# A new order for the slots of the first layer: lane transpositions, gates by Tanh, the middle layer's bank and the routing's norm

## The chip, the core and the metric

The kernel runs on one core of a Trainium2 chip. A core has a matrix engine (TensorE, PE in the profile; PEld is its weight load, which overlaps), VectorE (DVE), ScalarE (ACT), GpSimd (POOL) and SyncE (SP), each with an instruction stream of its own that it works off in order; semaphores tie the streams together. The metric is the time of one execution on the device in microseconds.

## The reference

The input is 4096 tokens of 128 numbers in float32. They pass two layers. Cut to what matters:

```python
# first layer
x = x + 0.5 * L0_ffn(layernorm(x))      # experts in LoRA form over shared weights
x = x + L0_attn(layernorm(x))
x = x + 0.5 * L0_ffn(layernorm(x))
# second layer
x = x + 0.5 * L1_ffn(layernorm(x))      # every token goes to one of 8 experts
x = x + L1_attn(layernorm(x))
x = x + 0.5 * L1_ffn(layernorm(x))

# L0_ffn: softmax over 8 experts, the best two; for each of them
h1 = t @ w1.T + 2 * (t @ a1[e].T) @ b1[e].T
h3 = t @ w3.T + 2 * (t @ a3[e].T) @ b3[e].T
act = silu(h1) * h3                     # weighted by the expert's share
out_e = act @ w2.T + 2 * (act @ a2[e].T) @ b2[e].T

# L0_attn: a recurrence along the sequence
h = layernorm(x) * g1 + b1;  f = sigmoid(h @ Wf + bf);  i = sigmoid(h @ Wi + bi)
o = sigmoid(h @ Wo + bo);    v = h @ Wv + bv
num = scan(f * num + i * v); den = scan(f * den + i)
x = x + o * num / (den + 1e-6)
m = square(leaky_relu((layernorm(x) * g2 + b2) @ W1 + b1));  x = x + m @ W2 + b2
```

(The reference writes the recurrence as an exponential of summed logarithms; the program computes it with scans.)

## The kernel before

The tokens lie in 8 chunks of 512. The first layer is a pipeline of slots (`Slot`, lines 52 to 63, `SLOTS`). Slot m does, for different chunks, one stage of each of many lanes. The main lane has 16 items, the 8 chunks for the first L0_ffn and again for the second: item m is `main` in slot m, `pre` (`q`, the transposition, the gate logits, the choice of the best two, the masks and the lane products `up`) in the slot before, `stat` two before, `tail` (`l`) one after. The attention's lanes lag: `a_stat` (slot m - 1), `a_pre`, `a_gate`, `a_norm`, `a_up`, `a_down` (m - 6) for chunks 0 to 7. The routing of the second layer lags more: `r_stat` (m - 9), `r_pre` (m - 10), `r_sort` (m - 11). So slots 0 to 2 hold only L0_ffn work beside statistics, slots 3 to 10 gates, 5 to 12 the middle layer, and 9 to 18 routing. Slots -2 and -1 fill the pipeline, 16 to 18 empty it; `fill` and `keep_busy` put products there whose results nobody uses.

Inside a slot the order of each engine is written out by hand: `first_layer(s)` stands once in each engine's block and ends with a list of calls. On TensorE, `h(1, k)` and `h(3, k)` (lines 362 to 364) are the products for h1 and h3, k = 1 to 8 for four column blocks and two experts, each of three or six split float32 products of 512 columns, which read `split` (the high and low halves of a float32). `value` (L421) is the product with `a2`, `down` (L431) the one with `w2`, `pre_T` (L358, `yn_f`), `logits` (L459), `mask` (L473, L476), `up` (L362) and `a_T` (L358, `yn_a`) belong to the lanes. `a_gate(i)` (L609) is one of four products of `hT` with the weights of i, f, o and v, all into one bank, `BSIDE`: gate i + 1 waits until gate i has been read. `a_den` (L502) and `a_back` (L358, `oaT`) belong to the attention of the slot before.

ScalarE applies Silu (L863), copies masks (L903), makes the high halves (`up_high`, L914), and reads the gates with Sigmoid (`a_gates`, L971). Its functions come from tables, and a change of table is an ACT_TABLE_LOAD. VectorE makes `act` (L1199, then L1203 by the expert's weight), `f_norm` (L1212: `yn_f`, at the head of the slot, for `q`), `masked` (L1266 and L1267: `ua`, `ud`), `a_leaky` (L1342), `a_scans` (L1360, L1361, L1363: `den`, `iv`, `num`) and the chains of small instructions for statistics, best two and routing. GpSimd adds the two experts' act (`total`, L1644), makes low halves (`low`, L1631; `up_low`, L1672), `mdT` (L1664), the inverse roots, `a_product` (L1709) and the scatter of the routing.

BSIDE (bank 5) is also the bank of the attention's transpositions, of `a_mid` (L573, the middle layer) and of the routing's affinities and ranks; BV (bank 4) holds `value` and the routing's transposition `r_T`; BPRE (bank 7) holds the lane's.

## Time and profile before

| | us |
|---|---|
| median of 3 runs | 1057.73 |
| lowest and highest | 1056.75, 1062.28 |
| the profiled execution | 1054.69 |
| its span, first to last instruction | 1053.0 |
| of it the first layer's slots | 0 to 684 |

The profile is of one execution, 3.0 us under the median. A row of its timeline is: start, length, engine, line, operation, output<-input, count, and in brackets how long the engine had been idle before it and what ended that. Matmuls are pipelined: the shown length of one overlaps the next, so the distance of two starts is the better measure of what one costs.

### The profile page before, as it was taken

How to read it: one execution, taken by the hardware profiler on the slowest of the kernel's cores; microseconds unless marked ns; L12 is line 12 of the kernel's file. 1: busy time of each engine (PE TensorE's matmuls, PEld its weight loads, DVE VectorE, ACT ScalarE, POOL GpSimd, SP SyncE). 2: the span in 40 equal slices, each digit the busy share in tenths (PEclk: the TensorE clock that was granted, in tenths of full speed). 3: DMA queues.
4: the chain of work that ended last, by engine and by line, in shares of the span. 5: the costliest groups of instructions: out<-in, count | busy, mean ns of one | idle time of the engine just before them, and what ended most of it. 6: DMA issues, size and time to landing. Idle time of an engine off the chain costs nothing. (4 is left out here: it accounts for less than half of the span.)

```text
span 1053.0 us, 15574 instructions
## 1 busy us (share of the span) xinstructions
PE 980.6 (93%) x4429; PEld 669.9 (64%) x4429; DVE 711.2 (68%) x2140; ACT 507.9 (48%) x1039; POOL 500.1 (47%) x485
## 2 busy tenths in 40 slices
PE   3999999999999999999999999899988999889993
PEld 2766667656565665656566656477864667648873
DVE  5787779788786877879797776445543667634542
ACT  3433454655646556564453332144534777515451
POOL 3456555554535545354654655524451155423443
PEclk9999999999999999999999999999999999989997
DMA  6069000000000000000000002146534000015651
GB/s 181 1 284 415 3 1 1 1 1 1 1 0 2 0 1 1 1 0 1 12 3 9 11 11 71 39 137 197 166 94 140 1 22 22 22 42 178 194 174 34
DMA packets 42900, 65.12 MB, mean 62 GB/s; under 512 B 7153, under 2 KB 25121, under 8 KB 40640
## 3 DMA queue, kind: packets, MB, share of 16 engines
q1 hardware_dynamic: 37824, 55.59, 16.1%
q0 software_dynamic: 4992, 8.54, 2.4%
q8 instruction: 36, 0.59, 0.2%
q14 instruction: 48, 0.39, 0.1%
HBM read 37.20 MB, written 28.74 MB: 63 GB/s over the span
## 5 line engine op out<-in xcount | busy, mean ns | idle before, releaser
L362 PE MATMUL bank<-split 128*128 128x512 f32 x416 | 206.9, 497 | 7.8 <-DVE ud L1267 4.1
L364 PE MATMUL bank<-split 128*128 128x512 f32 x416 | 165.2, 397 | 0.0
L363 PE MATMUL bank<-split 128*128 128x512 f32 x416 | 164.8, 396 | 0.0
L863 ACT ACTIVATE sil<-bank 128x512 f32<-128x512 f32 x128 | 76.2, 595 | 116.0 <-PE bank L364 115.2
L1644 POOL TENSOR_TENSOR gsum<-act 128x512 f32<-128x512 f32 x64 | 84.9, 1327 | 81.5 <-DVE act L1203 81.4
L421 PE MATMUL bank<-act,a 128*128 128x512 f32 x256 | 117.6, 592 | 0.0
L362 PEld LDWEIGHTS bank<-split 128*128 128x128 f32 x416 | 79.5, 191 | 48.8 <-issue 17.4
L1199 DVE TENSOR_TENSOR act<-bank,sil 128x512 f32<-128x512 f32 x128 | 87.8, 686 | 17.2 <-PE bank L364 14.2
L363 PEld LDWEIGHTS bank<-split 128*128 128x128 f32 x416 | 79.9, 192 | 28.3 <-issue 18.6
L688 PE MATMUL bank<-xlT,e 128*128 128x256 f32 x368 | 91.2, 392 | 5.1 <-ACT xlT L1068 2.7
L1203 DVE TENSOR_TENSOR act<-act,wT 128x512 f32<-128x512 f32 x128 | 91.7, 716 | 4.4
L364 PEld LDWEIGHTS bank<-split 128*128 128x128 f32 x416 | 79.2, 190 | 18.1
L704 PE MATMUL bank<-hT_e,e 128*128 128x256 f32 x368 | 87.3, 380 | 1.1 <-DVE oT_e L1534 1.1
L1068 ACT ACTIVATE xlT<-bank,lnb,lng 128x256 f32<-128x256 f32 x46 | 25.9, 564 | 119.0 <-PE bank L696 119.0
L1747 POOL DMA_INDIRECT rows_in<-yw,slot_i x64 | 62.9, 983 | 34.7 <-issue 18.8
L688 PEld LDWEIGHTS bank<-xlT,e 128*128 128x128 f32 x368 | 67.9, 194 | 16.5 <-issue 4.5
L1754 POOL DMA_INDIRECT out<-ob,ids x46 | 45.2, 983 | 66.9 <-DVE ob L1542 57.1
L1754 POOL DMA_INDIRECT rows_out<-ob,ids x46 | 45.2, 983 | 63.4 <-DVE ob L1542 55.6
L421 PEld LDWEIGHTS bank<-act,a 128*128 128x128 f32 x256 | 47.5, 190 | 42.0 <-issue 33.7
L704 PEld LDWEIGHTS bank<-hT_e,e 128*128 128x128 f32 x368 | 66.7, 191 | 8.7 <-issue 1.5
L431 PE MATMUL bank<-gsum,w 128*128 128x512 f32 x128 | 65.2, 600 | 0.5 <-POOL gsum L1644 0.5
L1529 DVE TENSOR_SCALAR hT_e<-bank,eb1T 128x256 f32<-128x256 f32 x92 | 40.3, 479 | 27.6 <-PE bank L688 27.2
(283 smaller groups left out, 1957.6 us busy)
## 6 DMA issues: line engine op xcount, KB each, us to landing
e<-e_dram SPq DMA_DIRECT2D x92, 256.0 KB, 3.1
rows_in<-yw SPq DMA_DIRECT2D x17, 1056.0 KB, 17.8
xin<-rows_in SPq DMA_DIRECT2D x46, 132.0 KB, 3.0
x<-rows_out SPq DMA_DIRECT2D x8, 256.0 KB, 4.7
rows_in<-yw,slot_i POOLq DMA_INDIRECT x64, 2.3
rows_out<-ob,ids POOLq DMA_INDIRECT x46, 2.3
out<-ob,ids POOLq DMA_INDIRECT x46, 2.4
act<-b_dram SPq DMA_DIRECT2D x2, 256.0 KB, 3.1
```

Source lines behind the costliest of these rows:

```text
L362: mm(dst, w[0], m[0], start=start, stop=False, **more)
L363: mm(dst, w[0], m[1], start=False, stop=False, **more)
L364: return mm(dst, w[1], m[0], start=False, stop=stop, **more)
L421: last = mm(bank[BV][:, :], a2[:, j, :], act_[e][j][:, :], start=j == 0, stop=j == J - 1)
L431: mm(bank[BOUT][:, :], w2[:, j, :], gsum[j % 2][:, :], start=j == 0, stop=False).then_inc(w2_used.sem, 1)
L688: last = mm(bank[2 * p + j // 2][:, (j % 2) * Q:(j % 2 + 1) * Q], w[:, rows(j)], xlT[p][:, :], start=True, stop=True)
L704: last = mm(bank[4][:, 0:Q], w[:, j, :], hT_e[p][:, j, :], start=j == 0, stop=j == J - 1)
L863: af(sil[(k - 1) % 2][:, :], bank[BH1[STEPS[k - 1][0] % 2]][:, :], ACT.Silu).then_inc(silu_done.sem, 1)
L1199: v.tensor_tensor(a[:, :], bank[BH3[j % 2]][:, :], sil[(k - 1) % 2][:, :], ALU.mult).then_inc(act_done.sem, 1)
L1203: v.tensor_tensor(a[:, :], a[:, :], wT[g % 2][e][:, :], ALU.mult).then_inc(weighted.sem, 1)
L1644: pool.tensor_tensor(out=gsum[j % 2][:, :], in0=act_[0][j][:, :], in1=act_[1][j][:, :], op=ALU.add).then_inc(summed.sem, 1)
L1754: pool.indirect_dma_start((rows_out, o)[n3 // NT], bass.IndirectOffsetOnAxis(ids[n3 % 4][:, q:q + 1], 0), ob[n3 % 4][:, q, :], None, bound ...
```

## The change

The lists of calls at the end of `first_layer` are written in a new order on all four engines, with the waits that this needs; three functions change.

- TensorE: `pre_T` between h(1,1) and h(3,1), `logits` after h(1,2), `a_den` after h(3,2), `a_back` after `value(1)`. The masks and the gates are spread over h(3,5) to h(3,8); `up(0)` after h(1,7), `up(1)` after h(1,8). `down(2)` and `down(3)` now end the slot, with no gates between them.
- The middle layer (`a_mid_T`, `a_mid`) moves from BSIDE to BV, the routing's `r_T` from BV to BSIDE. `r_T` then waits for what held BSIDE, `a_mid_T` for `r_done`; `value(0)` waits for `m_saved`, `r_rank` and `a_gate(0)` for `xnT_saved`.
- ScalarE: `a_gates` becomes `a_gate(i)`, called three times: the gate is 0.5 * tanh(0.5 * (z + b)) + 0.5, a Tanh out of the bank and a Copy in place. The halved biases are made once (`half`). `r_norm` of chunk n stands in slot n + 10 instead of n + 9, but for the last chunk.
- VectorE: `f_norm` leaves the head of the slot, works on `stat` and stands after act(8) and `a_leaky(1)`, so at the end of the slot before. `masked(0)` stands before act(7) and `masked(1)` before act(8). `r_rows` follows `f_norm`, `first_values` follows the scans.
- GpSimd: `up_low(0)` ahead of `total(2)`, `a_mid_scale` ahead of `total(0)`.

No instruction of TensorE is added or removed. On ScalarE each gate gets one Copy more.

```diff
@@ tensor: first_layer
                     if e == 0 and js[0] == 0:
                         pe.wait_ge(*r_done(g - 1))
-                        if s.r_pre is not None:
-                            pe.wait_ge(*xnT_saved(s.r_pre))
+                        if s.a_up is not None:
+                            pe.wait_ge(*m_saved(s.a_up))
...
+                    pe.wait_ge(*r_done(l))
+                    transpose4(BV, lambda t: h2[:, t, :]).then_inc(h2T_ready.sem, 1)
...
                     pe.wait_ge(*normed_r(n))
-                    pe.wait_ge(*r_done(MAINS - 1 if l is None else l))
-                    transpose4(BV, lambda t: yn4[n % 4][:, t, :]).then_inc(ynT_r.sem, 1)
+                    transpose4(BSIDE, lambda t: yn4[n % 4][:, t, :]).then_inc(ynT_r.sem, 1)
...
-                    mm(bank[BSIDE][:, :], wm1[:, rows(j)], h2T[:, :], start=True, stop=True).then_inc(m_ready.sem, 1)
+                    mm(bank[BV][:, :], wm1[:, rows(j)], h2T[:, :], start=True, stop=True).then_inc(m_ready.sem, 1)
...
-                h(1, 1); h(3, 1)
+                h(1, 1)
+                pre_T()
+                h(3, 1)
                 a_T()
                 h(1, 2)
+                logits()
...
+                a_gate(2)
                 h(3, 8)
                 value(0, (0, 1))
-                a_gate(0)
-                if q != 0:
-                    up(1)
+                a_gate(3)
                 value(0, (2, 3))
-                a_gate(1)
                 down(2)
-                a_gate(2)
                 down(3)
-                a_gate(3)
@@ scalar: first_layer
-                def a_gates():
+                def a_gate(i):
                     n = s.a_gate
                     if n is None:
                         return
+                    dst = (gi, gf, go)[i]
                     act.wait_ge(*oa_ready(n - 1))
-                    for i, (dst, bias) in enumerate(((gi, bif[:, 0:1]), (gf, bif[:, 1:2]), (go, vecs[:, 5:6]))):
-                        act.wait_ge(*gates_ready(n, i + 1))
-                        af(dst[:, :], bank[BSIDE][:, :], ACT.Sigmoid, bias=bias).then_inc(gates_saved.sem, 1)
+                    act.wait_ge(*gates_ready(n, i + 1))
+                    af(dst[:, :], bank[BSIDE][:, :], ACT.Tanh, bias=half[:, i:i + 1], scale=0.5).then_inc(gates_saved.sem, 1)
+                    act.wait_ge(*gates_saved(n, i + 1))
+                    af(dst[:, :], dst[:, :], ACT.Copy, scale=0.5, bias=0.5).then_inc(gates_done.sem, 1)
...
                 a_norm(0)
-                if s.a_gate is not None:
+                if s.m <= MAINS:
                     r_norm(s.r_pre)
...
+                a_gate(0)
+                silu(7)
+                a_mid(1)
+                a_gate(1)
+                a_mid(2)
                 silu(8)
                 up_high(0)
+                a_gate(2)
+                up_high(1)
+                a_square(0)
                 a_square(1)
                 a_square(2)
-                a_gates()
-                up_high(1)
                 a_norm(1)
-                if s.a_pre is None:
+                if s.m >= MAINS:
                     r_norm(s.r_stat)
@@ vector: first_layer
                 def f_norm():
-                    if q is None:
-                        return
-                    p = q % 2
-                    dve.wait_ge(*rstd_f(q))
-                    dve.wait_ge(*ynT_f(q - 1))
+                    n = s.stat
+                    if n is None:
+                        return
+                    p = n % 2
+                    dve.wait_ge(*rstd_f(n))
+                    dve.wait_ge(*ynT_f(n - 1))
...
                 a_leaky(0)
+                masked(0)
                 act(7)
+                masked(1)
+                act(8)
                 a_leaky(1)
+                f_norm()
                 r_rows(s.r_sort, BSIDE)
-                masked(0)
-                act(8)
                 a_leaky(2)
-                masked(1)
+                a_scans()
                 first_values()
-                a_scans()
@@ gpsimd: first_layer
                 r_scale(s.r_stat)
+                up_low(0)
                 total(2)
                 total(3)
-                up_low(0)
                 up_low(1)
                 a_product()
```

TensorE at the end of slot 7, before. bank 4 takes `value`, bank 5 the gates, bank 6 the down products, banks 0 and 2 h(1,1) and h(3,1) of the next slot, bank 7 the lane:

```order
L609 MATMUL bank5<-hT,wf_b 128x512
L431 MATMUL bank6<-gsum0,w2 128x512
L609 MATMUL bank5<-hT,wo 128x512
L431 MATMUL bank6<-gsum1,w2 128x512
L609 MATMUL bank5<-hT,wv 128x512
L362 MATMUL bank0<-split 128x512
L363 MATMUL bank0<-split 128x512
L364 MATMUL bank0<-split 128x512
L362 MATMUL bank0<-split 128x512
L363 MATMUL bank0<-split 128x512
L364 MATMUL bank0<-split 128x512
L362 MATMUL bank2<-split 128x512
```

The same place in the changed kernel, from the last gate on:

```order
L609 MATMUL bank5<-hT,wv 128x512
L421 MATMUL bank4<-act02,a2 128x512
L421 MATMUL bank4<-act03,a2 128x512
L431 MATMUL bank6<-gsum0,w2 128x512
L431 MATMUL bank6<-gsum1,w2 128x512
L362 MATMUL bank0<-split 128x512
L363 MATMUL bank0<-split 128x512
L364 MATMUL bank0<-split 128x512
L362 MATMUL bank0<-split 128x512
L363 MATMUL bank0<-split 128x512
L364 MATMUL bank0<-split 128x512
L358 MATMUL bank7<-ident,yn_f 128x128 x4
```

The gates for f and o have left this place for earlier ones in the slot, and the lane's transposition has come in front of bank 2.

VectorE at the same seam, before (r1 is `first_values`, act00 the first act of the next slot):

```order
L1199 TENSOR_TENSOR act13<-bank3,sil1 128x512
L1203 TENSOR_TENSOR act13<-act13,wT11 128x512
L1342 SCALAR_TENSOR_TENSOR msq2<-msq2 128x512
L1266 TENSOR_TENSOR ua1<-bank7,mT00 128x512
L1267 TENSOR_TENSOR ud1<-bank7,mdT 128x512
L1282 TENSOR_TENSOR r1<-bank4,mT10 128x512
L1360 SCALAR_TENSOR_TENSOR den<-gf,gi 128x512
L1361 SCALAR_TENSOR_TENSOR iv<-bank5,vecs,gi 128x512
L1363 SCALAR_TENSOR_TENSOR num<-gf,iv 128x512
L1212 TENSOR_SCALAR yn_f<-x,mv_f1,sc_f1 128x128 x4
L1199 TENSOR_TENSOR act00<-bank2,sil0 128x512
```

And in the changed kernel, where each line has moved down by 9 or 10:

```order
L1276 TENSOR_TENSOR ua1<-bank7,mT00 128x512
L1277 TENSOR_TENSOR ud1<-bank7,mdT 128x512
L1208 TENSOR_TENSOR act13<-bank3,sil1 128x512
L1212 TENSOR_TENSOR act13<-act13,wT11 128x512
L1352 SCALAR_TENSOR_TENSOR msq1<-msq1 128x512
L1222 TENSOR_SCALAR yn_f<-x,mv_f1,sc_f1 128x128 x4
L1352 SCALAR_TENSOR_TENSOR msq2<-msq2 128x512
L1370 SCALAR_TENSOR_TENSOR den<-gf,gi 128x512
L1371 SCALAR_TENSOR_TENSOR iv<-bank5,vecs,gi 128x512
L1373 SCALAR_TENSOR_TENSOR num<-gf,iv 128x512
L1292 TENSOR_TENSOR r1<-bank4,mT10 128x512
L1208 TENSOR_TENSOR act00<-bank2,sil0 128x512
```

`yn_f` has moved from behind the scans to ahead of the third leaky and of the scans.

GpSimd in slot 7, before:

```order
L1680 TENSOR_TENSOR sc_a0<-sc_a0,neghalf 128x8
L1683 TENSOR_TENSOR nb_a0<-sc_a0,mv_a0 128x8
L1644 TENSOR_TENSOR gsum0<-act02,act12 128x512
L1644 TENSOR_TENSOR gsum1<-act03,act13 128x512
L1672 TENSOR_TENSOR split<-ua0,split 128x512
L1672 TENSOR_TENSOR split<-ud0,split 128x512
L1672 TENSOR_TENSOR split<-ua1,split 128x512
```

And in the changed kernel:

```order
L1690 TENSOR_TENSOR sc_a0<-sc_a0,neghalf 128x8
L1693 TENSOR_TENSOR nb_a0<-sc_a0,mv_a0 128x8
L1682 TENSOR_TENSOR split<-ua0,split 128x512
L1682 TENSOR_TENSOR split<-ud0,split 128x512
L1654 TENSOR_TENSOR gsum0<-act02,act12 128x512
L1654 TENSOR_TENSOR gsum1<-act03,act13 128x512
L1682 TENSOR_TENSOR split<-ua1,split 128x512
```

Two of the four low halves now stand ahead of the two sums that the last down products read.

## Rows read from the trace of the kernel before

**Rows 1.** The page, part 1: busy us (share of the span) and instructions.

```profile
PE 980.6 (93%) x4429; PEld 669.9 (64%) x4429; DVE 711.2 (68%) x2140; ACT 507.9 (48%) x1039; POOL 500.1 (47%) x485
```

**Rows 2.** Busy, slots 1, 7: length, PE, PEld, DVE, ACT, POOL, clock, DMA, GB/s.

```profile
61.30:93.60 32.30, 32.30 (x133) 21.73 (x132) 26.74 (x63) 11.59 (x21) 18.87 (x34) 1.00 1.01 417
291.00:335.80 44.80, 44.40 (x177) 27.86 (x176) 35.01 (x87) 26.53 (x47) 22.51 (x18) 1.00 0.00 1
```

**Rows 3.** PE's waits, 28 to 684 us: whom for, us, times, longest.

```profile
PE bank L362 <- DVE ud L1267: 4.1, 3, 1.6
PE bank L609 <- ACT gi L971: 3.6, 6, 1.5
...
PE bank L358 <- DVE denc L1312: 1.0, 2, 0.7
...
PE bank L431 <- POOL gsum L1644: 0.5, 1, 0.5
...
PE bank L362 <- POOL split L1672: 0.3, 1, 0.3
```

**Rows 4.** Timeline of PE, end of slot 7: value, gates, down products.

```profile
321.54 1.88 PE L421 MATMUL bank<-act,a 128*128 128x512 f32 x4
323.80 1.10 PE L609 MATMUL bank<-hT,wf_b 128*128 128x512 f32 x2 [0.38 <-ACT gi L971]
324.73 1.02 PE L431 MATMUL bank<-gsum,w 128*128 128x512 f32 x2
325.76 1.10 PE L609 MATMUL bank<-hT,wo 128*128 128x512 f32 x2
326.70 1.02 PE L431 MATMUL bank<-gsum,w 128*128 128x512 f32 x2
327.73 1.10 PE L609 MATMUL bank<-hT,wv 128*128 128x512 f32 x2
```

**Rows 5.** Timeline of ScalarE at the same place.

```profile
321.67 1.28 ACT L971 ACT_TABLE_LOAD   x1
322.96 0.69 ACT L971 ACTIVATE gi<-bank,bif 128x512 f32<-128x512 f32 x1
```

**Rows 6.** Timeline of VectorE: the start, slot 0, the seam of slots 7 and 8.

```profile
6.76 1.11 DVE L1212 TENSOR_SCALAR yn_f<-x,mv_f,sc_f 128x128 f32<-128x128 f32 x4 [1.24 <-POOL sc_f L1657]
...
25.86 4.15 DVE L1212 TENSOR_SCALAR yn_f<-x,mv_f,sc_f 128x128 f32<-128x128 f32 x4
...
47.54 1.04 DVE L1203 TENSOR_TENSOR act<-act,wT 128x512 f32<-128x512 f32 x1
...
328.92 1.63 DVE L1360 TENSOR_TENSOR_SCAN den<-gf,gi 128x512 f32<-128x512 f32 x1 [4.77 <-PE bank L609]
330.47 0.72 DVE L1361 SCALAR_TENSOR_TENSOR iv<-bank,vecs,gi 128x512 f32<-128x512 f32 x1
331.22 1.50 DVE L1363 TENSOR_TENSOR_SCAN num<-gf,iv 128x512 f32<-128x512 f32 x1
```

**Rows 7.** Timeline of GpSimd: start, slot 0, the seam of slots 7 and 8.

```profile
26.19 1.27 POOL L1672 TENSOR_TENSOR split<-ud,split 128x512 fp32r<-128x512 f32 x1
27.42 1.27 POOL L1672 TENSOR_TENSOR split<-ua,split 128x512 fp32r<-128x512 f32 x1
...
46.73 1.30 POOL L1664 TENSOR_TENSOR mdT<-mT 128x512 f32<-128x512 f32 x1 [0.16 <-ACT mT L903]
...
328.18 1.28 POOL L1672 TENSOR_TENSOR split<-ua,split 128x512 fp32r<-128x512 f32 x1 [3.60 <-ACT split L914]
```

**Rows 8.** Timeline of PE in slot 0: h(1,1), h(3,1), h(1,2).

```profile
26.28 0.80 PE L362 MATMUL bank<-split 128*128 128x512 f32 x1 [3.34 <-POOL split L1672]
...
27.73 0.63 PE L362 MATMUL bank<-split 128*128 128x512 f32 x1
...
31.57 0.50 PE L362 MATMUL bank<-split 128*128 128x512 f32 x1
```

**Rows 9.** Groups by line: count, busy us, mean ns, idle before.

```profile
L1203 DVE TENSOR_TENSOR act<-act,wT 128x512 f32<-128x512 f32 x128 | 91.7, 716 | 4.4
```

104 lines of the change are left out of this document (52 added, 52 removed).

## The prediction

> **What bounds the kernel now.** I read the page's busy shares first: TensorE (PE) is busy 93% of the span [rows 1]. The table of busy time by stretch says where that holds. Slot 1, with no attention work in it, is 32.3 us with PE busy 32.30; slot 7, with every attention lane in it, is 44.8 us with PE busy 44.40, VectorE 35.01, ScalarE 26.53 and GpSimd 22.51 [rows 2]. So the first layer (0 to 684 us) is a row of PE instructions, and the edit adds and removes none of them. What it can change is the time in which PE stands still, and where. The list of PE's waits from 28 to 684 us gives what there is to win: 4.1 us for `ud`, 3.6 us for the gate `gi`, 1.0 for `denc`, 0.5 for `gsum`, 0.3 for a split [rows 3]. That list undercounts, since a matmul's shown length overlaps the next one's: I therefore also compare the distance of starts with the 0.855 us that a float32 product of 512 columns (two rows) takes; two value products show 1.88 and one down product 1.02, a difference of 0.86 [rows 4]. I write T for the end of h(3,8), the last product of a slot's main chunk.
>
> **What is removed.**
> (a) Gates, slots 3 to 10. In slot 7 the four value rows start at 321.54 and should end at 323.25, the second gate starts at 323.80: 0.55 lost, behind a table load of 1.28 us and the first Sigmoid [rows 4, 5]. The next four starts are 0.93, 1.03, 0.94 and 1.03 apart where 0.855 is the work: 0.51 more. So 1.07 in slot 7; five slots are alike, slot 5 loses 2.2, slots 3 and 4 about 0.6 and 0.9: 9.1 us. With Tanh the table stays; the build of the changed kernel has 3 table loads and the one before 19. With the gates spread, each has other PE work between it and the next. ScalarE also gets some 20 us back (16 loads x 1.28), which are worth nothing in themselves, since it is idle for 18 us of slot 7 [rows 2]. I take -9.1.
> (b) `masked(0)` now stands ahead of act(7) and `r_rows`, and the second lane product up(1) after h(1,8): the three waits for `ud` go. a_back behind value(1) loses its wait for `denc`, h(3,1) the one for a split. That is 5.4 us as listed and 6.7 by distance of starts. In slots 13 and 14 `r_stats` still stands ahead of `masked(0)`; I count that return below.
> (c) Slot 15: act(8) ahead of `r_rows` takes the wait of 0.54 for `gsum` (0.7 by starts) off the way to the tail. Together (b) and (c): -7.4.
>
> **What is added.** Two mechanisms.
>
> (d) The start. pre_T, the transposition of the next chunk, now stands between h(1,1) and h(3,1). In slot 0 it needs `yn_f` of chunk 1, which VectorE makes at 25.86 for 4.15 us, until 30.01 [rows 6]; its place there hardly moves. h(1,1) ends at 27.7 [rows 8], so PE stands for 2.4 us in the new order, where it now runs h(3,1). PE is slow there: split products start 0.43 apart until 31.57, after that 0.23 (the levels of 1.2 and 2.4 GHz); it had worked without a gap from 26.28 on. With a gap at 27.7-30.1 I expect the rise later: as an estimate three to four products more than before run at the lower level, 0.20 us each, 0.7 us. I take +3.1, bounds 2.4 (the wait alone) and 3.5.
>
> (e) VectorE and GpSimd get in each other's way. f_norm (four TENSOR_SCALAR) takes 1.11 us with GpSimd idle and 4.15 us beside a row of GpSimd instructions, which start 1.23 us apart, and it then ends with one of them (26.19 + 3 x 1.23 = 29.9) [rows 6, 7]: each piece waits for one. Before, it stood at the head of the next slot and nobody needed it until pre_T, some 4.5 us later. Now it follows act(8), and GpSimd has just then up_low(0), total(2), total(3), up_low(1) in a row: six instructions x 1.23. Behind it on VectorE wait leaky(2), the scans and `first_values`; for these wait, on PE, a_T (`iv` must have read the bank) and pre_T, and on ScalarE the third square, behind which `yn_a` and the next silu and `tT` stand. The multiply by `wT` with two SBUF inputs suffers too: 1.04 instead of 0.69 us beside GpSimd's `mdT` [rows 6, 7].
> A slot 5 to 9, walked with these lengths: act(8) T+0.2, its multiply held by the second split (until T+2.0) ends T+2.5; total(2) to 3.75; leaky(1) 4.3; total(3) 5.5; f_norm ends T+8.3 to 8.6; leaky(2), as long as the multiply, +0.6; `den` scan +1.55, `iv` +0.75 [rows 6, 9]: T+11.4. PE meanwhile: four value products 3.44 (twice two), gate 0.87, two down products 1.74, h(1,1) 1.4, pre_T 0.4, h(3,1) 1.4 [rows 4, 8]: a_T could start at T+9.3. It waits 2.1, plus 0.2 at a_out, behind the mixing on VectorE. If the multiply isn't held, the same walk ends with `iv` at T+10.4 (1.2 lost), and if neither it nor leaky(1) is held, at T+9.9 (0.65). I take 2.0, nearer to the first, since the held multiply is in the trace: 5 slots x 2.0 = +10.0, bounds 0.8 and 2.5.
> Slots 3, 4 and 10 lack leaky or `yn_a` and lose 0.6 each (0 to 1.2): +1.8.
> Slots 0, 1, 2, 13, 14 have no gates between value and the down products, so PE reaches down(2) at T+3.4 when total(2), now behind up_low(0), ends at T+3.7 (free) or T+4.3 (multiply held), then down(3) and pre_T in the same way: 0.7 or 1.75 a slot. I take 1.5: 5 x 1.5 = +7.5. Before, none of these waits exist.
> Slots 11 and 12 have leaky, the row numbers of the routing and no gates: 0.95 to 2.4 for the same waits, and 0.75 to 0.9 more at the logits, because the third square holds up silu(1) and `tT`. I take 2.8: 2 x 2.8 = +5.6, bounds 1.7 and 3.3.
>
> Edits at no cost: the early logits (VectorE reaches top2(0) late anyway), the middle layer's bank (free between second_values and value(0)), the norm for the routing a slot later (ScalarE has 18 us to spare in slot 7 [rows 2]), the three Copy instructions of 0.6 us, r_T behind the bank of the side work. If ScalarE were full, the last two would delay silu(8) and with it h(3,8). In the tail (slots 16 to 18) the order is as before; r_rank there waits for `xnT` besides, under four filling products.
>
> **Sum.** 3.1 - 9.1 - 7.4 + 10.0 + 1.8 + 7.5 + 5.6 = +11.5 us. The profiled execution took 1054.69 us with a span of 1053.0; with the sum it would be 1066.2. The median of the runs shown is 1057.73, 3.0 above it, and I put the sum on that: 1069.2. With all low bounds the sum is 2.4 - 16.5 + 4.0 + 0 + 3.5 + 3.4 = -3.2, with all high ones 3.5 - 16.5 + 12.5 + 3.6 + 8.8 + 6.6 = +18.5.
>
> The rows show f_norm and one kind of multiply waiting for GpSimd. The Trainium skill (SBUF — State Buffer, section "Who interferes with whom") says more: an instruction of VectorE with two SBUF inputs, or in a 2-port mode, and a GpSimd instruction exclude each other for the whole of the one that came first. By that rule the multiply and both leaky instructions are held in every slot, and the sum would be near the high end, +17. The trace agrees for the multiply (0.35 us of delay), but the `den` scan, which also has two such inputs, began 0.54 us before the end of a GpSimd split and took only 1.63 against 1.50 us for the other scan [rows 6, 7]: that speaks against the whole of the rule. Hence 2.0 and 1.5 above, not the high ends.
>
> **Rivals.**
> A, main, 0.46: the port between VectorE and GpSimd makes a new wait at the seam of each slot, larger than what the gates gave back. +6 to +18, forecast +11.5.
> B, 0.27: only f_norm is held. The walk gives about -3 to +3, so 1054 to 1061. For it: multiplies with their ordinary 0.69 us are the great majority (mean 0.716 [rows 9]); against it: few of them met a large GpSimd instruction.
> C, faster, 0.15: GpSimd's row starts earlier than I think, since ScalarE, free of table loads, delivers the high parts sooner; then f_norm meets two instructions and not four, all of (e) falls away but the order of the down products, and the sum is 3.1 - 16.5 + 4 = -9, 1048.5. It decides if up_low(0) is done by T+1.
> D, slower than the main case, 0.12: one more GpSimd instruction ahead of f_norm at each of twelve seams, 12 x 1.23 = 15 us on top of +11.5: 1084. It decides if f_norm ends after T+9.5.
> That the gates still wait (the spread order not doing what it says) I give no case of its own: every gate but the last has at least 1.5 us of other PE work ahead, ScalarE needs 0.7.
>
> **How the numbers follow.** 0.5% (5.3 us) is about what a measurement of this kernel can tell from no change. Faster by more: C and a little of B, 0.17. Slower by more: A nearly whole and D, 0.58. Within: 0.25. The range runs from the low part of B and C's upper edge to above A: 1050 to 1078; D and most of C are left out.
>
> **What would show it.** Right: PE rows of pre_T and a_T at the head of slots 6 to 10 with an idle time before them of 1 to 2 us, released by VectorE; f_norm of 4 us or more in most slots; down(2) and down(3) released by `gsum` in slots 0 to 2; h(3,1) of slot 0 starting near 31 us; no wait for `gi`, none for `ud` before slot 13. Wrong: slots of 43.5 us or less in the middle, f_norm of about 2 us there, or a seam at which PE waits for ScalarE.

## The result, and the profile after

The changed kernel is slower. Its median is 1076.54 us (1074.67 to 1078.36, 4 runs) against 1060.01 us for the kernel before (1056.75 to 1062.53, 4 runs); the ratio is 1.0158, with a 95% interval from 1.0118 to 1.0197. The profiled execution took 1075.88 us, its span is 1074.1 us.

Part 1 of the page of the changed kernel answers [rows 1]:

```profile
PE 981.6 (91%) x4429; PEld 669.4 (62%) x4429; DVE 742.9 (69%) x2140; ACT 493.2 (46%) x1049; POOL 500.5 (47%) x485
```

TensorE does the same work in a longer span. VectorE has the same 2140 instructions as before and is busy 32 us longer, 742.9 against 711.2. That is the first sign: instructions that became longer by standing beside others. The groups by line of VectorE, in the changed kernel (count, busy us, mean ns, idle before), show which:

```profile
L1212 DVE TENSOR_TENSOR act<-act,wT 128x512 f32<-128x512 f32 x128 | 111.4, 870 | 4.4
L1222 DVE TENSOR_SCALAR yn_f<-x,mv_f,sc_f 128x128 f32<-128x128 f32 x64 | 69.5, 1145 | 1.2 <-POOL sc_f L1667 1.2
L1352 DVE SCALAR_TENSOR_TENSOR msq<-msq 128x512 f32<-128x512 f32 x24 | 24.9, 1038 | 0.0
```

The multiply by `wT` went from a mean of 716 ns [rows 9] to 870, f_norm (64 pieces) to 1145, leaky to 1038. What this does to TensorE stands in the list of its waits from 28 to 700 us (whom for, us in total, times, longest), which answers [rows 3]:

```profile
PE bank L358 <- DVE yn_f L1222: 7.0, 11, 2.1
PE bank L431 <- POOL gsum L1654: 5.1, 9, 0.7
PE bank L377 <- ACT wak L849: 3.9, 1, 3.9
PE bank L358 <- ACT yn_a L987: 3.8, 5, 0.8
PE bank L522 <- DVE z L1335: 2.3, 1, 2.3
PE bank L459 <- ACT split L876: 1.0, 2, 0.6
PE bank L535 <- DVE z L1335: 0.9, 1, 0.9
```

No wait for `gi` or `ud` is left of those in [rows 3]. In their place stand pre_T's wait for `yn_f`, eleven times, the down products' wait for `gsum`, nine times, a_T's for `yn_a`, five times, and two for `z`. Slot 7, from one `tT` to the next, is now 45.63 us long with PE busy 44.38 (length, PE, PEld, DVE, ACT, POOL, clock, DMA, GB/s), where [rows 2] had 44.80 and 44.40:

```profile
294.79:340.42 45.63, 44.38 (x178) 27.98 (x177) 37.13 (x87) 24.85 (x49) 22.23 (x18) 1.00 0.00 1
```

The wait of 3.9 us for `wak` is at the end of the first layer and has nothing to do with the change: the run before_again, below, settles that.

### The profile page after: what moved, and what is told of

It reads as the page before. It is cut to its first block and busy times, and to the rows that moved or that the text cites. A ratio compares the mean times of both kernels' runs of the same rounds, so it can differ in the third digit from the quotient of the medians.

```text
span 1074.1 us, 15600 instructions
## 1 busy us (share of the span) xinstructions
PE 981.6 (91%) x4429; PEld 669.4 (62%) x4429; DVE 742.9 (69%) x2140; ACT 493.2 (46%) x1049; POOL 500.5 (47%) x485
## 5 line engine op out<-in xcount | busy, mean ns | idle before, releaser
L1212 DVE TENSOR_TENSOR act<-act,wT 128x512 f32<-128x512 f32 x128 | 111.4, 870 | 4.4
L1654 POOL TENSOR_TENSOR gsum<-act 128x512 f32<-128x512 f32 x64 | 91.3, 1436 | 38.5 <-DVE act L1212 38.3
L690 PE MATMUL bank<-xlT,e 128*128 128x256 f32 x368 | 88.7, 384 | 7.2 <-issue 4.5
L431 PE MATMUL bank<-gsum,w 128*128 128x512 f32 x128 | 67.4, 610 | 6.9 <-POOL gsum L1654 5.1
L1222 DVE TENSOR_SCALAR yn_f<-x,mv_f,sc_f 128x128 f32<-128x128 f32 x64 | 69.5, 1145 | 1.2 <-POOL sc_f L1667 1.2
## 6 DMA issues: line engine op xcount, KB each, us to landing
rows_in<-yw SPq DMA_DIRECT2D x17, 1056.0 KB, 17.9
```

The lines of the kernel that those rows point to most:

```text
L690: last = mm(bank[2 * p + j // 2][:, (j % 2) * Q:(j % 2 + 1) * Q], w[:, rows(j)], xlT[p][:, :], start=True, stop=True)
L1212: v.tensor_tensor(a[:, :], a[:, :], wT[g % 2][e][:, :], ALU.mult).then_inc(weighted.sem, 1)
L1222: last = v.tensor_scalar(yn_f[:, t, :], xc(n)[:, t, :], mv_f[p][:, t:t + 1], sc_f[p][:, 1, t:t + 1], ALU.subtract, ALU.mult)
L1654: pool.tensor_tensor(out=gsum[j % 2][:, :], in0=act_[0][j][:, :], in1=act_[1][j][:, :], op=ALU.add).then_inc(summed.sem, 1)
```

## The experiments

Twelve kernels ran. Each ratio is to the kernel before on the same chip. To place a gain or a loss I use one mark per slot, the start of down(0) on TensorE (the first row of the matmul with `w2` inside the slot), since the same amount of work stands before it in every kernel, but for two masks (0.6 us) that the changed kernel puts ahead of it in slots 0 to 14; slot 15 prepares no chunk and has no masks. Us from the start of the span:

| slot | before_again | changed | lane_old | fnorm_early | low_back | fnorm_act | preT_late |
|---|---|---|---|---|---|---|---|
| 0 | 42.61 | 46.52 | 42.73 | 46.32 | 46.76 | 45.99 | 43.86 |
| 3 | 139.86 | 149.56 | 139.93 | 147.54 | 143.02 | 146.06 | 145.53 |
| 5 | 218.28 | 227.67 | 216.42 | 225.63 | 220.18 | 225.69 | 225.46 |
| 10 | 444.91 | 457.10 | 434.28 | 450.15 | 450.31 | 447.86 | 458.59 |
| 11 | 491.55 | 507.22 | 478.95 | 495.91 | 500.59 | 498.18 | 508.73 |
| 13 | 571.13 | 590.96 | 556.60 | 576.95 | 587.12 | 579.38 | 594.14 |
| 15 | 640.67 | 658.52 | 622.11 | 644.03 | 652.59 | 646.62 | 661.58 |

### The execution of before that was profiled: before_again

> The kernel before, unchanged, for a second profile. All nine other profiles show a pause of 4 us before the matmul of line 377, the one profile of the kernel before does not, and that execution was 3 to 4 us under the median of its own runs. If the pause belongs to most executions of every kernel, this profile shows it too and lasts about 1058 us; then 4 of the 21 us between the two spans are no effect of the change. If the pause depends on the program, it is not here, and the execution takes 1055 us.

The ratio was 1.000 (0.999 to 1.001), the profiled execution took 1058.22 us with a span of 1056.5. Its list of waits has the pause, as do the profiles of all other kernels here. The wait of the matmul of line 377 there, and the two starts around it in the timeline of TensorE:

```profile
PE bank L377 <- ACT wak L847: 3.9, 1, 3.9
```

```profile
672.64 0.22 PE L375 MATMUL bank<-ident,eb1r 32*128 32x32 f32 x1
676.79 0.49 PE L377 MATMUL bank<-wak,wq_l 128*128 128x128 f32 x2 [3.93 <-ACT wak L847]
```

So the one profile on which the prediction rested came from an execution without that pause, 3 us under its median. The two spans, 1053.0 and 1074.1, differ by 21.1 us, of which 3.9 are the pause. In the first layer the two executions of before are 1.1 us apart since slot 0 (the clock, below), and that distance stays to 0.2 us. What is to be explained is the distance at slot 15: 658.52 - 640.67 = 17.9 us.

### Only Tanh: tanh_only

```diff
-                    for i, (dst, bias) in enumerate(((gi, bif[:, 0:1]), (gf, bif[:, 1:2]), (go, vecs[:, 5:6]))):
+                    for i, dst in enumerate((gi, gf, go)):
                         act.wait_ge(*gates_ready(n, i + 1))
-                        af(dst[:, :], bank[BSIDE][:, :], ACT.Sigmoid, bias=bias).then_inc(gates_saved.sem, 1)
+                        af(dst[:, :], bank[BSIDE][:, :], ACT.Tanh, bias=half[:, i:i + 1], scale=0.5).then_inc(gates_saved.sem, 1)
+                    for i, dst in enumerate((gi, gf, go)):
+                        act.wait_ge(*gates_saved(n, i + 1))
+                        af(dst[:, :], dst[:, :], ACT.Copy, scale=0.5, bias=0.5).then_inc(gates_done.sem, 1)
```

> The kernel before with one thing of the change: the gates read with Tanh and a Copy, in their old place and order; nothing else moves. It prices the gates by themselves. My step (a): the first gate's wait in the slots with gates (0.55 us in slots 7 to 11, 1.7 in slot 6) sits behind a table load and goes; the spacing of the other gates (0.51 us a slot above the work) comes from reading the bank and stays while gates and down products alternate. So about 4.5 us faster than before, ratio 0.996. If the table load is also behind the spacing, the whole 9.1 us of the prediction show here: 0.991. Rival: the six hundred nanoseconds of each Copy stand in ScalarE's queue ahead of the high halves and of yn_a, and PE waits for those instead: ratio 1.000 or above.

The ratio was 1.001 (1.0000 to 1.0019), as the rival said. The waits for `gi` are gone from TensorE's list, and this one is new in it:

```profile
PE bank L362 <- POOL split L1678: 5.2, 9, 0.6
```

3.6 us were won and 5.2 given back. The three Copies stand ahead of up_high(1) on ScalarE, so the last low half is late for h(1,1). Tanh alone, in this order, is worth nothing.

### Tanh, Copies later, r_rows later: tanh_rows2

```diff
                 a_gates()
                 up_high(1)
+                gate_copies()
@@ vector
-                r_rows(s.r_sort, BSIDE)
                 masked(0)
                 act(8)
                 a_leaky(2)
                 masked(1)
+                r_rows(s.r_sort, BSIDE)
```

> The kernel before with Tanh gates in their old place as in tanh_only, but up_high(1) stands ahead of the three Copies, and r_rows behind act(8), leaky(2) and masked(1). In tanh_only the waits for gi (3.6 us) were gone and waits of h(1,1) for split (5.3 us in nine slots) had come, behind the Copies. If the Copies' place was the cause, these go, and the waits for ud (4.1 us) go with r_rows: 7 us less than before at the end of the first layer. Of that, 4 us are lost again if the pause before the matmul of line 377, that every kernel with Tanh shows so far, stays: ratio 0.997 with it, 0.993 without it.

The ratio was 0.9986 (0.9974 to 0.9999), which is 1.5 us and not 7. The waits for `split` and `ud` went as expected, but the Copies, now behind up_high(1), make the gates and so the scans late:

```profile
PE bank L358 <- DVE iv L1373: 7.0, 7, 1.0
```

Of the two positions tried for the Copies in the old place of the gates, neither is free.

### f_norm off VectorE: fnorm_act

```diff
@@ scalar
                 up_high(1)
+                f_norm()      # yn_f = sc_f * x + nb_f, four ACTIVATEs of 128x128
                 a_square(0)
@@ vector
                 a_leaky(1)
-                f_norm()
@@ gpsimd: f_scale
+                    pool.tensor_tensor(nb_f[n % 2][:, :], sc_f[n % 2][:, 1, :], mv_f[n % 2][:, :], ALU.mult).then_inc(rstd_f.sem, 1)
```

> The changed kernel with f_norm on ScalarE (four ACTIVATEs of 128x128, about 1.65 us, behind up_high(1)) instead of on VectorE; GpSimd makes one more small product for its bias. This takes the 4 us of VectorE beside GpSimd out of the seam of the slots and leaves everything else in place. Theory A (VectorE and GpSimd in each other's way): the waits of PE for yn_f (7.0 us in eleven places) go, those for yn_a (3.8) and z (3.2) nearly go since leaky(2) and the scans stand 4 us earlier, and the multiply and leaky(1) stay long. About 12 us faster than the changed kernel, 8 to 16, ratio to before 1.000 to 1.008. Rival: f_norm is long only because it has nothing to hurry for, and the late multiply is what holds the seam: 3 us or less gained, ratio 1.013 or more.

The ratio was 1.0049 (1.0028 to 1.0069) against 1.0158 for the changed kernel: 1.1%, 11 to 12 us, as theory A expected. The waits for `yn_f` and `yn_a` are gone. Those for `z` stay, against the expectation, and `gsum` grew (5.1 us in the changed kernel):

```profile
PE bank L432 <- POOL gsum L1654: 7.0, 11, 0.9
PE bank L523 <- DVE z L1336: 2.0, 1, 2.0
```

### GpSimd's order put back: low_back

```diff
-                up_low(0)
                 total(2)
                 total(3)
+                up_low(0)
                 up_low(1)
```

> The changed kernel with GpSimd's order at the end of the slot put back: total(2), total(3), then up_low(0), up_low(1). Theory A (two GpSimd instructions ahead of the totals make down(2) and down(3) late in slots without gates): the nine waits for gsum, 5.1 us, go, and f_norm on VectorE stays at 4 us because GpSimd's row has the same length; about 5 us faster than the changed kernel, ratio to before 1.011. Rival: the low halves of the lane become late in their place and h(1,1) of the next slot waits for split, or pre_T's wait grows by what the down products give back: ratio 1.015 to 1.016, unchanged.

The ratio was 1.0098 (1.0081 to 1.0114), 6 us faster than the changed kernel. The nine waits for `gsum` went and the marks gain 7.5 us by slot 5; but in slots 5 to 12 f_norm now lasts 5.0 us instead of 4.0, and a_T waits longer:

```profile
PE bank L358 <- ACT yn_a L987: 8.9, 5, 1.8
```

Of the 7.5 us, 1.6 are given back by slot 15 (652.59 against 658.52). In slots 11 and 12 TensorE's granted clock fell to its lower level once more each, at 522.1 and 566.5 us, where it did not in the changed kernel; from the mark of slot 11 to that of slot 13 this kernel loses 2.8 us of its lead. A mere exchange of two GpSimd instructions changes the length of a VectorE instruction by a microsecond.

### pre_T behind h(3,1): preT_late

```diff
                 h(1, 1)
-                pre_T()
                 h(3, 1)
                 a_T()
+                pre_T()
                 h(1, 2)
@@ scalar
                 silu(1)
-                pre_T()
                 a_T()
+                pre_T()
```

> The changed kernel with one move undone on PE and ScalarE: pre_T stands behind h(3,1) and a_T instead of ahead of h(3,1). If the waits for yn_f (2.1 us in slot 0, 1.85 in slot 1, 0.5 in slot 2, 0.3 in nine later ones) are real losses, h(3,1) covers them: start 2.5 to 3.2 us less, slot 1 about 1.4 to 2.0 less, slot 2 0.7, nine slots 0.4 each; a_T's wait for yn_a grows by the same 0.4 in five of these. Sum about 7 us faster than the changed kernel, ratio to before 1.009. Rival: VectorE's next act is late as well, so the wait only moves on to a_T, value or the logits: 2 us or less gained, ratio 1.014 or more.

The expected 7 us did not come: the ratio was 1.0187 (1.0165 to 1.0210), its interval overlaps that of the changed kernel, and at the mark of slot 15 it is 3.1 us behind. The start did gain, 43.86 against 46.52 at the mark of slot 0. Later the wait moved on: a_T waits 1.7 us instead of 0.8 in slots 6 to 10, about its old wait, pre_T's 0.3 and pre_T itself (0.45) together, and the logits, now only h(1,2) behind pre_T, wait for ScalarE:

```profile
PE bank L358 <- ACT yn_a L987: 8.7, 5, 1.8
PE bank L459 <- ACT split L876: 3.7, 10, 1.1
```

So in the slots with attention the early pre_T is not the cause but only the first to feel it. The chain on VectorE and ScalarE is late.

### a_mix ahead of the second choice: mix_first

```diff
                 a_den()
+                a_mix()
                 top2(1)
                 split_low(LOW_DVE[2:])
                 second_values()
-                a_mix()
```

> The changed kernel with one move on VectorE: a_mix stands right behind a_den again, ahead of top2(1) and second_values. In the changed kernel PE waits 2.33 us for z in slot 11 and 0.9 twice at the head of other work; VectorE makes z there only after the second choice of the best two and second_values, some 2.8 us of instructions. If that order is the cause, the wait falls to below 1 us and the kernel is about 2.5 us faster than the changed one, ratio to before 1.0135. Rival: z is late because everything on VectorE is late by the 4 us of f_norm, then the wait goes on to second_values and value(0) and nothing is gained: 1.016.

Both expectations fell: the ratio was 1.0312 (1.0283 to 1.0342), 16 us worse than the changed kernel. Of the waits for `z` one of 0.7 us is left, and instead:

```profile
PE bank L439 <- POOL r L1660: 9.1, 8, 3.2
```

a_mix needs a_back, and in the changed kernel a_back stands behind the four value products. Placed early, a_mix blocks VectorE's queue until then; top2(1) and second_values, and behind them GpSimd's sum of the values, come late. Placed late, it is itself late. With a_back behind value(1) neither of the two places tried for a_mix is good.

The loss is not spread evenly. At the mark of slot 3 this kernel is 1.2 us behind the changed one, at that of slot 5 12.4: 11.2 us arise in slots 4 and 5, the first with a_mix, where TensorE waits 3.2 us for `r` each time. Around each of these two waits the granted clock falls to its lower level for longer than anywhere in the changed kernel's middle; this row is from the first of them (length, PE, PEld, DVE, ACT, POOL, clock, DMA, GB/s):

```profile
184.00:188.00 4.00, 3.94 (x7) 2.50 (x8) 3.85 (x8) 0.60 (x1) 3.60 (x4) 0.50 0.01 2
```

So 6.4 of the 11.2 us are the waits, and most of the rest fits what followed them at half the clock.

### Four repairs at once: combined

This is fnorm_act with the edits of low_back and mix_first, and pre_T behind h(3,1) in slot 0 alone.

> The changed kernel with four repairs at once: f_norm on ScalarE, up_low(0) behind total(3), a_mix behind a_den, and in slot 0 alone pre_T behind h(3,1). If the causes are separate, their gains add: 11 (measured for f_norm), 7 (measured for the low halves), 2.5 and 2.5 off the changed kernel's 1076.5, so about 1053 or a ratio to before of 0.995. If low_back's gain was the same time as f_norm's (both shorten the same seam), 1058 to 1060, ratio 1.000.

The ratio was 1.0094 (1.0077 to 1.0111): worse than fnorm_act alone. It carries mix_first's loss (`r`, 9.1 us again, two of the waits 3.2 us), and the low halves, behind the totals and behind ScalarE's f_norm, are late for h(1,1): `split` is listed with 8.8 us, of which 3.6 are the wait at the start that every kernel has (3.3 in the kernel before [rows 8]) and 5.2 in eight slots are new. These four repairs did not add up, and one of them, a_mix, was no repair.

### Ten instructions more: pad

```diff
+                        for z_ in range(10):
+                            af(pad[:, 2 * z_:2 * z_ + 2], bif[:, :], ACT.Copy, scale=0.5)
```

> The kernel before with ten tiny ACTIVATEs (128x2) more on ScalarE, in slot 2 where it has time, so that ScalarE's program has as many instructions as with the Tanh gates. It asks after the pause of 4 us at the end of the first layer, between the matmuls of lines 375 and 377, which all five kernels with Tanh show and the kernel before does not. If it comes from where ScalarE's instructions lie in its program, it shows here: about 3.7 us slower, ratio 1.0035. If it has to do with Tanh or the missing table loads, it doesn't: 1.000.

The profile shows the pause (4.1 us), but the ratio was 1.0011 (0.9996 to 1.0026), not 1.0035. At this point it looked as if the place in ScalarE's program mattered; before_again showed that the unchanged kernel has the pause as well, so it is not tied to the added instructions.

### The lane in its old place: lane_old

```diff
@@ tensor: first_layer (against the changed kernel)
                 h(1, 1)
-                pre_T()
                 h(3, 1)
                 a_T()
                 h(1, 2)
-                logits()
+                a_den()
                 h(3, 2)
-                a_den()
-                value(1, range(J))
+                pre_T()
                 a_back()
+                value(1, range(J))
...
                 h(3, 3)
+                logits()
@@ vector: end of the slot
-                masked(0)
                 act(7)
-                masked(1)
-                act(8)
                 a_leaky(1)
-                f_norm()
-                r_rows(s.r_sort, BSIDE)
+                masked(0)
+                act(8)
                 a_leaky(2)
-                a_scans()
+                masked(1)
+                r_rows(s.r_sort, BSIDE)
                 first_values()
+                a_scans()
```

f_norm stands at the head of the next slot, the masks and up(0) one step later, top2, a_mix and GpSimd's totals as before.

> The changed kernel with the lane of the next chunk back in its old places: f_norm at the head of the next slot, pre_T behind h(3,2), logits, masks and up as before, a_mix behind act(2), GpSimd's totals ahead of the low halves. Kept from the change: Tanh, the gates spread over h(3,6) to h(3,8), the middle layer in its own bank, a_norm of the routing a slot later, r_rows behind act(8). If the loss sits in the moves of the lane (the new waits at the seam) and the gains in the spread gates, this keeps the gains alone: the waits for gi and ud (7.7 us) and most of the gates' spacing go, no wait for yn_f, gsum or z comes back; 1048 to 1053 us, ratio 0.990 to 0.995. Rival: VectorE's and ScalarE's work of a slot is tight enough that any order pays at the seam (as with iv in tanh_rows2): ratio 0.998 to 1.003.

It did better than expected: 1041.32 us median (1038.22 to 1045.72), ratio 0.9826 (0.9800 to 0.9853). It is faster than both kernels. Slot 7 has no idle time at all on TensorE (columns as above):

```profile
288.00:331.48 43.48, 43.48 (x179) 28.20 (x177) 35.62 (x88) 25.38 (x48) 23.19 (x18) 1.00 0.00 1
```

And the three kinds of instruction on VectorE are short again:

```profile
L1210 DVE TENSOR_TENSOR act<-act,wT 128x512 f32<-128x512 f32 x128 | 91.8, 717 | 4.4
L1220 DVE TENSOR_SCALAR yn_f<-x,mv_f,sc_f 128x128 f32<-128x128 f32 x64 | 48.4, 844 | 1.3 <-POOL sc_f L1665 1.2
L1350 DVE SCALAR_TENSOR_TENSOR msq<-msq 128x512 f32<-128x512 f32 x24 | 16.4, 684 | 0.0
```

### One move put back in: fnorm_early

```diff
@@ vector: first_layer (against lane_old; f_norm takes s.stat instead of s.pre)
-                f_norm()
                 r_factors(s.r_pre)
...
                 act(8)
+                f_norm()
                 a_leaky(2)
                 masked(1)
```

> The kernel lane_old with one move of the change put in: f_norm, on VectorE, stands behind act(8) at the end of the slot before, as in the changed kernel, while pre_T keeps its late place and GpSimd its old order. If VectorE beside GpSimd is the cause, f_norm grows from 2 to 3 us to 4 to 5 us there, leaky(2), masked(1) and the scans come that much later, and PE waits at the seam for iv or yn_a or split, 1 to 2 us in slots 4 to 12: 8 to 18 us slower than lane_old, ratio to before 0.990 to 1.000. Rival: f_norm early does no harm by itself, only PE's early pre_T made it one: within 3 us of lane_old, ratio 0.983 to 0.986.

1061.41 us median, ratio 1.0019 (0.9999 to 1.0040): against lane_old some 20 us slower, more than the 8 to 18 expected, from one call moved on VectorE. The seam of slots 7 and 8, VectorE, then GpSimd:

```profile
327.11 4.01 DVE L1220 TENSOR_SCALAR yn_f<-x,mv_f,sc_f 128x128 f32<-128x128 f32 x4
331.04 0.68 DVE L1350 SCALAR_TENSOR_TENSOR msq<-msq 128x512 f32<-128x512 f32 x1
```

```profile
327.27 1.32 POOL L1652 TENSOR_TENSOR gsum<-act 128x512 f32<-128x512 f32 x1 [2.75 <-DVE act L1210]
328.55 1.26 POOL L1680 TENSOR_TENSOR split<-ua,split 128x512 fp32r<-128x512 f32 x1
329.78 1.26 POOL L1680 TENSOR_TENSOR split<-ud,split 128x512 fp32r<-128x512 f32 x1
```

f_norm begins as GpSimd begins its row and ends as the third of it ends (327.11 + 4.01 = 331.12 and 329.78 + 1.26 = 331.04). Behind it are leaky(2), masked(1) and the scans, and TensorE waits for what they feed:

```profile
PE bank L362 <- POOL split L1680: 8.9, 7, 1.5
PE bank L358 <- DVE iv L1369: 5.5, 7, 0.9
```

By the marks, the middle slots cost (450.15 - 225.63) - (434.28 - 216.42) = 6.7 us in five slots, 1.33 each, and the start 3.6; at slot 15 it is 21.9 us behind lane_old. This isolates the early f_norm as a cause: no PE instruction is moved here. It does not by itself part the place from the length: of the 4.01 us, 1.11 are what four unheld pieces take [rows 6], and the other 2.9 are the holding. In lane_old, at the head of the slot, f_norm is held too (3.0 us in slot 7), but nobody waits for it there.

### The spread gates with Sigmoid: sig_spread

```diff
-                    af(dst[:, :], bank[BSIDE][:, :], ACT.Tanh, bias=half[:, i:i + 1], scale=0.5).then_inc(gates_saved.sem, 1)
-                    act.wait_ge(*gates_saved(n, i + 1))
-                    af(dst[:, :], dst[:, :], ACT.Copy, scale=0.5, bias=0.5).then_inc(gates_done.sem, 1)
+                    af(dst[:, :], bank[BSIDE][:, :], ACT.Sigmoid, bias=(bif[:, 0:1], bif[:, 1:2], vecs[:, 5:6])[i]).then_inc(gates_saved.sem, 1)
```

> The kernel lane_old with Sigmoid for its gates again (no Copy), all else alike, the gates spread between the silus. It tells the share of Tanh from that of the spread order. Each gate now costs two table loads of 1.28 us, six in a slot instead of two in the kernel before, 7.7 us of ScalarE where it had some 18 us to spare. If ScalarE's spare time covers them, the gates' gain is that of the order and the ratio stays 0.983 to 0.986. If not, h(1,8), value(0) and the gates wait for silu and gi, by 1 to 3 us a slot in eight slots: ratio 0.990 to 1.005.

1068.66 us, ratio 1.0091 (1.0058 to 1.0124), 27 us slower than lane_old, a little beyond the range. The masks and the gates wait for ScalarE:

```profile
PE bank L476 <- ACT mT L903: 10.6, 8, 2.0
PE bank L609 <- ACT go L971: 9.4, 8, 1.3
```

So neither half of the gates' change does it alone: Tanh in the old order brings nothing (tanh_only), the new order with Sigmoid costs 27 us against the same order with Tanh, and both together bring the gain of lane_old. (lane_old also keeps the middle layer's new bank and the later norm of the routing; their share was not separated.)

## Why the prediction was right, point by point

The forecast was 1069.2 us, 11.5 over before, in a range of 1050 to 1078; measured are 1076.5, 16.5 over and 1.5 under the upper edge. lane_old has the gains without the moves of the lane, so lane_old against before_again measures (a) and (b), and the changed kernel against lane_old measures (d) and (e), by the marks, where the 0.6 us of the two masks is taken off (d) and given back in the last seams, since slot 15 has none. lane_old puts r_rows behind act(8), which the changed kernel does in another way; the parts are therefore good to about a microsecond.

| step | predicted | measured |
|---|---|---|
| (a) gates, slots 3 to 10 | -9.1 | -11.1 |
| (b) waits for `ud`, `denc`, a split | -6.7 | -7.5 |
| (c) the wait for `gsum` in slot 15 | -0.7 | behind the last mark |
| (d) start | +3.1 | +3.2 |
| (e) seams 0, 1, 2 | +4.5 | +5.8 |
| (e) seams 3, 4 | +1.2 | +1.6 |
| (e) seams 5 to 9 | +10.0 | +11.6 |
| (e) seam 10 | +0.6 | +5.5 |
| (e) seams 11, 12 | +5.6 | +6.1 |
| (e) seams 13, 14 | +3.0 | +2.7 |
| sum | +11.5 | +17.9 |

The wait of (c) is gone from the changed kernel, but one of 0.5 us for `r` stands close behind it. The working: lane_old is 18.6 us ahead of before_again at slot 15 (640.67 - 622.11), of which 12.6 arise by slot 11; 1.5 of these are `denc` in slots 10 and 11 and belong to (b). The changed kernel is behind lane_old by 3.8 at slot 0 (0.6 of it the masks), 9.6 at slot 3, 11.3 at slot 5, 22.8 at slot 10, 28.3 at slot 11, 34.4 at slot 13 and 36.4 at slot 15.

The start is the least certain row, since the clock rises at another time in every execution: at the mark of slot 0 the profiles with the changed kernel's start (this one, low_back, mix_first) stand at 46.5 to 47.6 us, those with the old start (both of before, tanh_only, tanh_rows2, pad, lane_old) at 42.6 to 43.8. Less the masks, (d) lies between 2.1 and 4.5.

**The mechanism of (e) was right, its price in part.** f_norm beside GpSimd lasts 4 us and more in every slot, and the seam of slots 10 and 11 shows all the other instructions that wait too. VectorE, changed kernel:

```profile
468.23 1.55 DVE L1212 TENSOR_TENSOR act<-act,wT 128x512 f32<-128x512 f32 x1
469.70 1.75 DVE L1352 SCALAR_TENSOR_TENSOR msq<-msq 128x512 f32<-128x512 f32 x1
471.37 4.03 DVE L1222 TENSOR_SCALAR yn_f<-x,mv_f,sc_f 128x128 f32<-128x128 f32 x4
475.32 0.68 DVE L1352 SCALAR_TENSOR_TENSOR msq<-msq 128x512 f32<-128x512 f32 x1
475.92 1.21 DVE L1370 TENSOR_TENSOR_SCAN den<-gf,gi 128x512 f32<-128x512 f32 x1
```

GpSimd in the same stretch:

```profile
467.96 1.27 POOL L1682 TENSOR_TENSOR split<-ud,split 128x512 fp32r<-128x512 f32 x1
469.18 3.39 POOL L1654 TENSOR_TENSOR gsum<-act 128x512 f32<-128x512 f32 x2
472.54 1.26 POOL L1682 TENSOR_TENSOR split<-ua,split 128x512 fp32r<-128x512 f32 x1
473.76 1.30 POOL L1682 TENSOR_TENSOR split<-ud,split 128x512 fp32r<-128x512 f32 x1
```

The multiply waits for the split of 467.96, leaky(1) for the first total, f_norm ends just after the last (475.06), and GpSimd's two totals last 3.39 instead of 2.5 us, which fits that they wait for VectorE in turn. By the walk f_norm was to end 8.3 to 8.6 us after the end of h(3,8); it ended 8.15 after (467.25 to 475.40). Of the signs named, these came: waits at pre_T, f_norm of 4 us or more, `gsum` in slots 0 to 2, h(3,1) of slot 0 at 31.01, no `gi`, no `ud`. Two did not. The idle time before pre_T and a_T was to be 1 to 2 us; listed are 0.3 and 0.8. And a_T was to be released by `iv` on VectorE; it was released by `yn_a` on ScalarE, a seam where PE waits for ScalarE, which the prediction had named as a sign of being wrong. `yn_a` stands behind the third square and so behind the same leaky(2), so the chain is the one meant. In slot 7 a_T starts 11.0 us after the end of h(3,8) (329.08 to 340.09); the walk had 11.4.

The price was 2.3 us a seam in slots 5 to 9 for 2.0, but f_norm is not all of it: fnorm_act takes back 1.45 a seam by the marks ((457.10 - 227.67) - (447.86 - 225.69) = 7.3 in five), and fnorm_early adds 1.33. Of the other 0.9, some 0.35 is the down products' wait for `gsum`: the four rows of down(2) and down(3) last 2.23 us in slot 7, too little for the list of waits, where lane_old has 1.88. The rest was not traced.

**The part that failed is seam 10**, "Edits at no cost: the early logits (VectorE reaches top2(0) late anyway)". top2(0) delays nobody, but with top2(1), second_values and first_values it now stands ahead of a_mix. In slot 11, the only one that has both r_aff and a_mix, r_aff needs `z`. VectorE there:

```profile
487.39 0.69 DVE L1262 TENSOR_TENSOR oh<-bank,mx 128x512 bf16<-128x512 f32 x1
488.00 0.15 DVE L1267 TENSOR_TENSOR dlt<-mx 128x4 f32<-128x4 f32 x1
488.07 0.68 DVE L1299 TENSOR_TENSOR r<-bank,mT 128x512 f32<-128x512 f32 x1
488.67 1.12 DVE L1335 SCALAR_TENSOR_TENSOR z<-bank,denc,ys 128x128 f32<-128x128 f32 x4
```

and TensorE:

```profile
489.94 0.25 PE L522 MATMUL bank<-cen,xnT 128*128 128x8 f32 x1 [2.33 <-DVE z L1335]
```

The prediction had costed what stood behind the moved instructions only up to top2(0), not down to the next one that PE needs. fnorm_act still has this wait (2.0), so f_norm is not its main cause; in mix_first it is down to 0.7, at the price told above.

The wait is only half of the loss, for the clock fell behind it. Two us of the profile after the wait, with the columns as above, and the granted clock at 0.50:

```profile
492.00:494.00 2.00, 2.00 (x4) 0.93 (x3) 1.49 (x3) 0.00 (x0) 1.22 (x2) 0.50 0.00 0
```

From r_aff to lora_out (L439) the changed kernel takes 7.27 us (489.94 to 497.21), lane_old 5.63 for the same work (463.25 to 469.69, less 0.81 for the logits, which stand there), so the lower level cost 1.6. With 2.5 for the wait by starts, 0.5 for `denc` and what the other seams lose too, this is the 5.5 of the table; 0.6 was predicted.

**The argument against the high end was wrong.** The prediction took 2.0 and 1.5 us where the rule of the Trainium skill (SBUF — State Buffer, "Who interferes with whom") gave the high ends, because the `den` scan of [rows 6] seemed hardly held: 1.63 us against 1.50 for the other scan. The other scan was no free baseline. Counted over all profiles of this case, the mean length of a VectorE instruction by the number of GpSimd instructions of 512 columns whose shown time overlaps with its own is (us, count in brackets):

| | 0 | 1 | 2 | 3 | 4 | 5 |
|---|---|---|---|---|---|---|
| f_norm, four pieces | 1.11 (12) | 2.06 (44) | 2.79 (22) | 4.24 (45) | 4.60 (60) | 5.00 (9) |
| `den` scan | 1.21 (29) | 1.54 (19) | 1.78 (64) | | | |
| `num` scan | 1.22 (40) | 1.49 (48) | 1.49 (24) | | | |
| multiply by `wT` | 0.69 (1408) | 0.99 (297) | 1.27 (82) | 1.83 (5) | | |
| leaky | 0.68 (175) | 0.78 (115) | 1.75 (46) | | | |
| act, one input out of a bank | 0.69 (1352) | 0.69 (380) | 0.69 (60) | | | |

A scan alone takes 1.21 us, so the `den` scan of [rows 6] had been held for 0.42, and the `num` scan that it was compared with for 0.28. The next row of GpSimd in the kernel before, which the prediction had not put beside it, says the same from the other side: this split has the length of one (1.26) and a wait of almost 1.0 for the scan.

```profile
329.42 2.22 POOL L1672 TENSOR_TENSOR split<-ud,split 128x512 fp32r<-128x512 f32 x1
```

The last line of the table fits the rule too: act, one of whose inputs is read from a bank, is never held. (f_norm, which has one tensor and two columns from SBUF and writes to SBUF, is held; no row here tells in which mode it runs, so which case of the rule it is stays open.)

On the length of the held instructions the trace agrees with the Trainium skill, and the doubt cost 3.1 us of the forecast: (e) without seam 10 and the seams 3 and 4 was put at 23.1 and measured 26.2. That the rule's sum, "near the high end, +17", is so close to the measured 17.9 is in part luck: seam 10 brought 4.9 us more for another reason, and the gains were 2.1 us larger than put.

**(a) was too small by 2 us.** The prediction took 1.07 us for each middle slot; lane_old is 1.4 to 1.6 us shorter in each from mark 6 to mark 9 (43.48 against 44.94 in the first). It comes only with Tanh and the spread together, which the prediction did not separate.

**The rivals.** B (only f_norm is held) falls with the rows of the multiply and of leaky. C (GpSimd's row starts early enough) falls with f_norm of 4 us in every slot. D (one more GpSimd instruction ahead at twelve seams) was not reached, though low_back shows its size: f_norm 5.0 instead of 4.0 in slots 5 to 9, and a_T's wait 1.0 longer there.

## What to carry to other kernels

Moving work on VectorE to a place that looks idle for the queue is not free when GpSimd has a row of large instructions there: count the instructions that read two tensors from SBUF and those that, like f_norm, go from SBUF to SBUF in short pieces, since every piece can wait for one GpSimd instruction. When a step is moved ahead, follow its queue down to the next instruction that another engine waits for, not only to the step itself, and expect that a long wait on TensorE costs more than itself, since its clock can fall behind it (here behind the 2.0 to 3.2 us for `z` or `r` in the changed kernel, low_back, preT_late, fnorm_act, mix_first and combined). And when a change bundles gains and losses, put its parts back one by one: here the same edits without the moves of the lane are 1.7% faster than before, while the whole is 1.6% slower.

## What the runs showed of the hardware

**A gap in TensorE's work at the start delays the rise of its clock by more than the gap.** At the granted clock of 1.2 GHz split products of slot 0 start 0.43 us apart, at 2.4 GHz 0.23. In before_again TensorE works without a gap from 26.23 us and the level rises at 29.3:

```profile
28.96 0.57 PE L362 MATMUL bank<-split 128*128 128x512 f32 x1
29.37 0.39 PE L363 MATMUL bank<-split 128*128 128x512 f32 x1
```

In the first profile of before it rose at about 31.7 [rows 8], in lane_old at 29.4: this alone sets two executions of one kernel 1.1 us apart. In the changed kernel, after a gap of 2.12 us at 28.1, it rises at 33.3, and in fnorm_early, after one of 1.30 us at 29.2, only at 35.4:

```profile
34.91 0.62 PE L363 MATMUL bank<-split 128*128 128x512 f32 x1
35.33 0.43 PE L364 MATMUL bank<-split 128*128 128x512 f32 x1
```

There the gap of 1.3 us cost 3.6 us at the mark of slot 0. Over all profiles: in the ten with no gap, or with one of 0.3 us (fnorm_act), the level rises 2.9 to 5.5 us after the first product of h(1,1), in the four with a gap of 1.3 to 2.1 us (the changed kernel, low_back, mix_first, fnorm_early) 6.8 to 9.6 us after it, which is 3.1 to 5.9 after the end of the gap.

**In the middle of the kernel a wait can bring the lower level back.** After the 2.33 us for `z` in slot 11 the distance of the split products goes from 0.23 to 0.43 us:

```profile
491.50 0.63 PE L363 MATMUL bank<-split 128*128 128x512 f32 x1
491.93 0.63 PE L364 MATMUL bank<-split 128*128 128x512 f32 x1
```

lane_old, fnorm_early and before_again, whose waits in slots 1 to 15 are shorter (none, 1.5 and 1.6 us at the longest), keep the upper level there. But the level also fell at places with only short waits before them (1.4 us in low_back at 522, 0.8 in tanh_rows2 at 474), so the length of one wait does not settle it.

**A pause of 3.7 to 4.1 us at the end of the first layer** stands in every profile but the first one of the kernel before. VectorE and ScalarE both see TensorE's signals late there (VectorE 5.57 us idle, with no releaser that the profile knows), while GpSimd goes on. It is not tied to Tanh, to the table loads or to ScalarE's number of instructions (pad and before_again have it alike). What it is stays open. For reading a comparison it means that two spans can differ by 4 us without any effect of the change: look at the same mark in both.
